# Attention merged into the expert layer without a lead, and the residual stores and loads issued by GpSimd instead of SyncE

## The reference

```python
def attn(h):                       # 8 heads of 64
    q, k, v = h @ Wq, h @ Wk, h @ Wv
    q = softmax(q, axis=head_dim) * SCALE
    k = softmax(k, axis=tokens)
    context = einsum('bhdn,bhen->bhde', k, v)
    return einsum('bhde,bhdn->bhen', context, q) @ Wo + bo
def ffn(u):                        # 16 routed and 2 shared matrices, dense
    g = top2_mask(softmax(u @ centroids.T + expert_biases))
    routed = einsum('bse,bseo->bso', g, einsum('bsd,eod->bseo', u, Wr) + br)
    shared = (einsum('bsd,eod->bso', u, Ws) + sum(bs)) / 2
    return u + routed + shared
x = x + ln(attn(ln(x)))
x = x + ln(ffn(ln(x)))
```

## Time and profile before

| what | us |
|---|---|
| two timed runs | 3109.3 and 3362.63, middle 3235.97 |
| the profiled execution, own time | 3081.65 |
| its span, slowest core (core 1) | 3080.0 |
| spans of the 8 cores | 3053.0 to 3080.0 |
| PE busy | 2441.9 (79%) |
| DVE busy | 1576.4 (51%) |

### The profile page before, as it was taken

The page is one execution under the profiler, slowest core; times in us unless marked ns, Lnnn a source line. Parts: engine busy times, 40 slices in busy tenths (PEclk is TensorE's granted clock), DMA queues, the critical chain, the costliest instruction groups (busy, mean ns, idle before and its releaser), DMA issues.

```text
span 3080.0 us, 38462 instructions; the slowest of 8 cores (3053.0 to 3080.0 us)
## 1 busy us (share of the span) xinstructions
PE 2441.9 (79%) x12014; PEld 1106.8 (36%) x12014; DVE 1576.4 (51%) x2882; ACT 113.0 (4%) x353; POOL 15.8 (1%) x29
## 2 busy tenths in 40 slices
PE   3243440459999999499999994999999949999994
PEld 1121220124444444144444441444444414444442
DVE  4132342656656644566566445665664454444445
ACT  0000000000000000000000000000000000000000
POOL 0000000000000000000000000000000000000000
PEclk9666675669999999799999997999999979999997
DMA  5989998213444433533444334334433343333334
GB/s 110 135 126 133 161 131 137 94 35 71 81 99 100 103 69 76 143 82 81 85 99 102 75 79 139 82 77 89 100 81 76 79 139 60 78 77 74 79 75 134
DMA packets 678005, 296.33 MB, mean 96 GB/s; under 512 B 632337, under 2 KB 643089, under 8 KB 676660
## 3 DMA queue, kind: packets, MB, share of 16 engines
q1 hardware_dynamic: 672628, 251.86, 35.0%
q0 software_dynamic: 5184, 42.01, 11.7%
HBM read 142.78 MB, written 79.69 MB: 72 GB/s over the span
## 4 chain that ended last, share of the span: by engine, by line
PE 66%; DVE 10%; DMA 9%; DVEq 5%; issue 3%; another core or an unknown queue 3%; SPq 3%; ACT 0%; POOL 0%; ACTq 0%; POOLq 0%
PE pb L897 57%; DMA xA<-xin 7%; SPq L79 3%; PE pb L800 2%; PE pb L842 2%; DVEq L426 2%; PE pb L886 1%; DVE ftmp L638 1%; DVEq L64 1%; DMA yld<-yscr 1%; DMA cen_st<-cen 1%; DVE att L537 1%; DVE ftmp L635 1%; PE pbT L854 1%
## 5 line engine op out<-in xcount | busy, mean ns | idle before, releaser
L897 PE MATMUL pb<-wrt,uT 128*128 128x512 bf16 x9216 | 2020.5, 379 | 4.8 <-DMA wrt<-wbf 3.3
L897 PEld LDWEIGHTS pb<-wrt,uT 128*128 128x128 bf16 x9216 | 894.3, 98 | 1074.7 <-issue 13.6
L612 DVE SCALAR_TENSOR_TENSOR racc<-pb,gAll,racc 128x512 f32<-128x512 f32 x1024 | 757.2, 749 | 820.4 <-PE pb L897 793.1
L742 PE MATMUL pbT<-eye,hb 128*128 128x128 bf16 x256 | 32.1, 306 | 228.1 <-DVEq L64 227.6
L612 DVE SCALAR_TENSOR_TENSOR racc<-pb,halfc,racc 128x512 f32<-128x512 f32 x128 | 96.1, 750 | 125.0 <-PE pb L897 125.0
L800 PE MATMUL pb<-wqb,hT 128*128 128x512 bf16 x240 | 66.2, 429 | 80.5 <-DVE racc L607 80.1
L854 PE MATMUL pbT<-eye,ub 128*128 128x128 bf16 x256 | 23.5, 246 | 124.4 <-DVEq L64 124.1
L742 PEld LDWEIGHTS pbT<-eye,hb 128*128 128x128 bf16 x256 | 24.8, 137 | 234.2 <-issue 234.0
L424 DVE BATCH_NORM_STATS2 Abn<-xA 128x6 f32<-128x512 f32 x32 | 22.2, 692 | 146.3 <-DMA xA<-xin 143.3
L463 DVE CAST vb<-pb 128x512 bf16<-128x512 f32 x32 | 22.2, 694 | 105.6 <-PE pb L769 80.7
L886 PE MATMUL pb<-eyeblk,uT 128*128 128x512 bf16 x256 | 71.7, 406 | 0.0
(11 more groups left out here) (109 smaller groups left out, 892.8 us busy)
## 6 DMA issues: line engine op xcount, KB each, us to landing
xA<-xin SPq DMA_DIRECT2D x128, 256.0 KB, 5.8
wbf<-wr POOLq DMA_DIRECT2D x16, 2048.0 KB, 37.3
wrt<-wbf SPq DMA_TRANSPOSE x1152, 2.8
yscr<-att SPq DMA_DIRECT2D x32, 512.0 KB, 4.0
yld<-yscr SPq DMA_DIRECT2D x32, 512.0 KB, 4.3
out<-ftmp SPq DMA_DIRECT2D x32, 512.0 KB, 2.9
hscr<-hT SPq DMA_DIRECT2D x32, 256.0 KB, 38.5
hT<-hscr SPq DMA_DIRECT2D x60, 128.0 KB, 4.8
```

Source lines behind the costliest of these rows:

```text
L612: ii = v.scalar_tensor_tensor(rsl, pb[bk][:], gcol, rsl, ALU.mult, ALU.add)
L742: last = pe.transpose(pT[:, kk * P:(kk + 1) * P], hb4[i4][:, kk * P:(kk + 1) * P], eye[:])
L897: last = pe.matmul(pb[bk][:], uT[:, kk * NTOK + tt * P:kk * NTOK + (tt + 1) * P], wrt[par][:, kk * HID:(kk + 1) * HID], start=(kk == 0), s ...
```

## The change

Two edits. `prop_merge` loses its lead: the first item of a stage is now one of attention, and the units (and the end of a quarter) are spread from there. And the store of y and the two loads of x for tile t+2 leave SyncE's queue: a loop at the end of GpSimd's program waits for each y in list order and issues the three. The semaphores are new ones (`dYg`, `dX2g`, `dX2gh`) for t >= 2 on the loads; the loads of h stay with SyncE, and no longer stand behind a wait for y.

```diff
-    def prop_merge(la, lb, lead=36):
+    def prop_merge(la, lb):
...
-        lead0 = min(lead, nb)
-        ib = lead0
-        outl.extend(lb[:ib])
-        ratio = (nb - lead0) / na
+        ratio = nb / na
+        ib = 0
...
-            want = min(nb, lead0 + int(round((ia + 1) * ratio * 0.65)))
+            want = int(round((ia + 1) * ratio * 0.65))
...
         if tag == "a2_v_y":
             t = it[1]; i = t % 2
-            em.wait(sync, "vA2", (t, "y"))
-            em.dma(sync, f"dY{i}", t, yscr[t * P:(t + 1) * P, :], att[i][:])
-            if t + 2 < NT:
-                em.dma(sync, f"dX2{i}", t + 2, xA[i][:, 0:HID],
-                       xin[(t + 2) * P:(t + 3) * P, 0:HID])
-                em.dma(sync, f"dX2h{i}", t + 2, xA[i][:, HID:D],
-                       xin[(t + 2) * P:(t + 3) * P, HID:D])
...
+        for it in flow_tail:
+            if it[0] != "a2_v_y":
+                continue
+            t = it[1]; i = t % 2
+            em.wait(gp, "vA2", (t, "y"))
+            em.dma(gp, f"dYg{i}", t, yscr[t * P:(t + 1) * P, :], att[i][:])
+            if t + 2 < NT:
+                em.dma(gp, f"dX2g{i}", t + 2, xA[i][:, 0:HID],
+                       xin[(t + 2) * P:(t + 3) * P, 0:HID])
+                em.dma(gp, f"dX2gh{i}", t + 2, xA[i][:, HID:D],
+                       xin[(t + 2) * P:(t + 3) * P, HID:D])
```

More of the change, by code:

```diff
@@ L409, in h_sync @@
             t = q * QT + j
-            em.wait(sync, f"dY{t % 2}", t)
+            em.wait(sync, f"dYg{t % 2}", t)
             if (q, j) not in ((0, 0), (0, 1)):
@@ L518, in h_vector @@
                 em.wait(v, "vA2", (t - 2, "ub"))
-                em.wait(v, f"dY{i}", t - 2)
+                em.wait(v, f"dYg{i}", t - 2)
             v.tensor_tensor(att[i][:, 0:512], pb[it[2]][:], boRep[:, 0:512], ALU.add)
@@ L534, in h_vector @@
             v.drain()
-            em.wait(v, f"dX2{i}", t)
-            em.wait(v, f"dX2h{i}", t)
+            if t < 2:
+                em.wait(v, f"dX2{i}", t)
+                em.wait(v, f"dX2h{i}", t)
+            else:
+                em.wait(v, f"dX2g{i}", t)
+                em.wait(v, f"dX2gh{i}", t)
             v.tensor_tensor(att[i][:], att[i][:], xA[i][:], ALU.add)
```

## The result

Over many runs the changed kernel takes 3119.55 us (median of 43), the kernel before 3098.11 (median of 42); the ratio is 1.007, 95% interval 1.0054 to 1.0086. It is slower by 0.7%, some 21 us: clear of noise, and far within the 2% that I called no change.

The account below looks back on a forecast made before the run. TensorE bounds the kernel from stage 1 on, VectorE stage 0 and the seams. Terms 0 + 0 + 0 + 15 - 1.5 = 13.5 us slower, added to 3081.65 and 3109.3, middle 3109 us; range 3070 to 3240.

Parts of the forecast that it names:

- Two softmaxes ... 6.6 us together, move into: Seams before stages 2 and 3: q's softmaxes and copies lengthen VectorE's stretch by 6.6 us, not filling its idle time.
- Shift of 4 us: Same two seams: TensorE has done its 7.5 us of work at about 1303.0, where before at 1299.2.
- 3.5 us for VectorE's backlog: After each of these seams: VectorE has 27 us of work, TensorE 20; transpose of u waits 3.5 us more.
- No lead, stage 1 ... 0, at worst 2 us: Start of stage 1: VectorE's copies are light and TensorE has units meanwhile, so losing the lead costs 0, at worst 2 us.
- A little more cover later: Stages after the start: more units per attention item shrink the small waits by a twentieth, 1.5 us back over three stages.
- Either end of a single transfer fits into 33 us, so the cost is 0: Store of y and loads of x on GpSimd: stage 0's slack covers a transfer of up to 6 us, cost 0.
- SyncE freed of the waits for y ... I take 0: SyncE's queue: loads of weights and h can go earlier; gain at most 1.6 us per stage, taken as 0.
- GpSimd's transfers hinder the transposing loads, a cost that I set at nothing: Sign of error: TensorE waiting for weights by tens of us; cost set at nothing.
- Rival A: Stage 0: GpSimd's transfers land late, 120 us of standing at three crossings, 3229 us; chance 0.11.
- Rival B: Seams and stages: early merge hides more than it costs, small waits halve, 20 us back, 3070 or 3097 us; chance 0.10.
- C: After the seams: VectorE behind for a whole pair, TensorE waiting 15 us per seam, 3134 us; chance 0.10.
- D: Whole kernel: freed queue, same landing times, a seam that only changes places, 3082 to 3109 us; chance 0.14.

Follow-up runs that it names:

- its control: The unchanged kernel before, run once more on another chip beside the repeat of the GpSimd edit alone: ratio 0.9996, stage sum +2.0 us.
- the two steps before: Kernel before with y's loads of first two tiles ahead of last half matrix: 0.9936; then also each tile's end behind its last unit: 0.9903.
- the control pair: Two repeats on another chip: the kernel before, unchanged, ratio 0.9996, and it with only the GpSimd edit (lead kept), ratio 1.0042.

## Why the prediction was right or wrong

**Direction and size.** I had 13.5 us more than the kernel before; measured are 20 by the stages and 21 by the runs. The written time, 3109 us, is 0.3% from 3119.55 and in its range. That closeness is in part luck: the middle of 3081.65 and 3109.3, to which I added my sum, happens to lie 3 us from the 3098.11 that the kernel before takes. And as a statement against the shown 3235.97 us it reads as a gain, and that came from how I tied my sum to two runs that lay far apart: a difference carried to a shown time that the kernel before does not usually take says the wrong sign. The difference was the forecast, and should have been given as that first.

**Point by point.**
- *"Two softmaxes ... 6.6 us together, move into" VectorE's stretch, and "can't fill the 11.35 us of idling".* Right. The seams grew by 5.6 and 6.3 us (alone: 5.5 and 6.3), and the idle time stayed at 10.3.
- *Shift of 4 us, and then 3.5 us for VectorE's backlog.* Right in sum: seam and next stage together +7.3 and +5.6 us for my 7.5 each; with no lead in stages 2 and 3 alone the whole is 12.6 us for my 15, less 1 of cover. The division between the two is not as I had it: the seam takes nearly all of VectorE's 6.6 us, and TensorE worked 11.0 us in it where I counted 7.5 (each product with the context takes 0.6 us where I had 0.7 for two, and the seam's granted clock was 0.57). The wait for the transpose of u rose from 4.4 to 8.9 us, by 4.5 where I took 3.5.
- *"No lead, stage 1 ... 0, at worst 2 us".* Wrong in size: 2.8 to 3.8 us. I looked at VectorE's light work among the units of s=0 and set the rest of the stage at nothing. The wait for the transpose of q went from 2.0 to 3.3 us, that of u from 7.7 to 10.4, in the first three tile pairs, which stand for the most part among full-length units; the fourth pair gained 2.0. Why it moves so stays open.
- *"A little more cover later", 1.5 us back.* Not shown as such: in stage 3 the kernels without the lead there are 0.7 to 1.3 us shorter, in stage 2 they are 0 to 1.7 longer, and the small waits for attention items grew.
- *"Either end of a single transfer fits into 33 us, so the cost is 0", and "SyncE freed of the waits for y ... I take 0".* In the median the transfers land as I took them (4.0 and 5.5 us; the longest load of x took 11.7, and nobody waited for it), stage 0 is unmoved, and the freed queue gave nothing that shows. This is the step that failed: the cost of 0 for GpSimd's queue. I asked who waits for these transfers and not what they run into. Their price is 5.6 us in the change, and 11.5 and 15.8 us alone (the second against its control). I had named the case among the signs of error ("GpSimd's transfers hinder the transposing loads, a cost that I set at nothing") without a price.
- *Rival A* (late transfers in stage 0, 120 us) did not come: nothing in stage 0 waits. The Trainium skill's port rule (SBUF — State Buffer, on two separate sides), that VectorE can hold GpSimd's descriptors back, shows in no median here: over the eight cores stores of y in stage 0 landed after 3.0 us from either queue. *Rival B* (small waits halved) is refuted, they grew. *C* (whose 25 us should read 23, two times 15 - 3.5) and *D* lie on either side of what came.

The error of the sum is then 20.3 - 13.5 = 7 us: about 3 of it the missing lead in stage 1 and about 5.6 GpSimd's queue, both of which I had at 0, less 2 that I had put too high in the seams.

## What to carry to other kernels

Before moving DMAs to an idle engine's queue, list what is in flight at the moment when they will start: one queue in program order also keeps big transfers out of the way of urgent ones, and nobody's wait shows that. A lead of independent work is worth what it covers: put it where it stands beside the stretch in which the other engine is the bound, not ahead of it (here the s=0 units among the tiles' ends: 2.5% with the two steps before, 1.5% beyond them). And when a lead is taken away, look at the waits of the whole stage, not of its start alone.

## What the runs showed of the hardware

- Weight loads that met transfers from a second queue took up to 14.0 us to land, where with one queue they had landed within 7.2 (stages 1 to 3); GpSimd's and ScalarE's queues did it alike.
- A wait of TensorE of 4.5 us, from 724.5 to 729.0, came with a stretch at the lower clock level (granted 0.50, 1.2 GHz, from 727.6 to 734.4), so such a wait costs more than its length: in the control pair there were 1 to 1.7 us of longer busy time beside 3 us of waits.
- The first pass, in which the DMA share is 0.79 to 0.92 (core 1, kernel before, up to 500 us), took 485 to 546 us on cores with the same program, and made most of the difference between spans.
